# One GpSimd instruction with immediate scalars ahead of the third sequence's gathers, and two VectorE blocks exchanged in the second step

## The reference, cut to what matters

```python
emb = wte[shifted ids]                 # 16 shifts, 64 numbers each
h = tanh(emb.reshape(.., 1024) @ w1 + b1)        # 64 columns
h = h @ w2 + b2                                  # 1024 columns ("logits")
h = h + attn(layernorm(h))             # autocorrelation, top 6 lags, softmax, shifted sums
h = h + layernorm(h) @ W.T + bias + low-rank update (16 experts of rank 16)
```

## Time and profile before

| | us |
|---|---|
| median of 3 runs | 404.94 |
| these three runs | 403.80, 404.94, 409.43 |
| the profiled execution, its own time | 404.97 |
| its span, first to last instruction | 403.1 |
| PE busy in the span | 382.9 (95%) |
| DVE busy | 276.5 (69%) |
| ACT busy | 246.3 (61%) |
| POOL busy | 214.2 (53%) |

### The profile page before, as it was taken

The page is one execution under the profiler, slowest core; times in us unless marked ns, Lnnn a source line. Parts: engine busy times, 40 slices in busy tenths (PEclk is TensorE's granted clock), DMA queues, the critical chain, the costliest instruction groups (busy, mean ns, idle before and its releaser), DMA issues.

```text
span 403.1 us, 6527 instructions
## 1 busy us (share of the span) xinstructions
PE 382.9 (95%) x1908; PEld 278.7 (69%) x1908; DVE 276.5 (69%) x602; ACT 246.3 (61%) x362; POOL 214.2 (53%) x283
## 2 busy tenths in 40 slices
PE   2999699999999999999999999999999999999992
PEld 1554377777777777777777777777777777777661
DVE  2745438686777778686858677777858686866751
ACT  2524267676766675776667676667677666764641
POOL 6774626657374737466574737473856654412200
PEclk9999879999999999999999999999999999999998
DMA  8783005455565555555545556554565554555575
GB/s 212 238 329 118 5 17 210 161 228 179 215 227 212 196 179 213 201 211 199 230 143 228 202 218 224 195 208 163 213 217 213 182 229 149 212 204 208 211 312 213
DMA packets 27684, 79.86 MB, mean 198 GB/s; under 512 B 6186, under 2 KB 7482, under 8 KB 27668
## 3 DMA queue, kind: packets, MB, share of 16 engines
q1 hardware_dynamic: 22960, 75.18, 48.4%
q0 software_dynamic: 4096, 4.20, 4.8%
q10 hardware_dynamic: 612, 0.27, 0.4%
HBM read 12.40 MB, written 67.12 MB: 197 GB/s over the span
## 4 chain that ended last, share of the span: by engine, by line
PE 85%; POOL 5%; issue 3%; DMA 2%; DVE 2%; ACT 0%; DVEq 0%; POOLq 0%
PE o_ps L1092 46%; PE conv_ps L1183 14%; PE o_ps L1118 7%; PE conv_ps L1189 7%; POOL gathered L403 4%; PE sum_ps L1157 2%; PE sum_ps L1131 2%; PE et_ps L1137 2%; PE mix_ps L1169 2%; PE sum_ps L1169 2%; PE et_ps L1147 2%; DMA gathered<-in_wte,idx_now 1%; DMA ids_sb<-in_ids 1%; DVE obuf L711 1%; PE conv_ps L1077 0%
## 5 line engine op out<-in xcount | busy, mean ns | idle before, releaser
L403 POOL DMA_INDIRECT gathered<-in_wte,idx_now x128 | 127.4, 996 | 44.2 <-issue 34.4
L511 ACT ACTIVATE obuf<-o_ps,mean_sb,a_sb 128x512 f32<-128x512 f32 x128 | 99.7, 779 | 74.8 <-PE o_ps L1118 46.5
L711 DVE TENSOR_SCALAR obuf<-o_ps,a_sb,mean_sb 128x512 f32<-128x512 f32 x128 | 102.4, 809 | 57.6 <-PE o_ps L1092 33.1
L1092 PE MATMUL o_ps<-w_hi,u_hi 128*128 128x512 f32 x256 | 110.2, 430 | 0.0
L1092 PE MATMUL o_ps<-w_lo,u_hi 128*128 128x512 f32 x256 | 101.2, 395 | 0.0
L1092 PE MATMUL o_ps<-w_hi,u_lo 128*128 128x512 f32 x256 | 101.2, 395 | 0.0
L1183 PE MATMUL conv_ps<-et_hl,shift_hi 128*128 128x512 f32 x256 | 67.0, 405 | 0.0
L1092 PEld LDWEIGHTS o_ps<-w_hi,u_hi 128*128 128x128 f32 x256 | 48.1, 188 | 21.2 <-issue 12.3
L1183 PEld LDWEIGHTS conv_ps<-et_hl,shift_hi 128*128 128x128 f32 x256 | 49.2, 193 | 12.8 <-issue 1.1
L431 POOL TENSOR_SCALAR var_eps<-var 128x8 f32<-128x8 f32 x16 | 3.1, 196 | 100.8 <-DVE var L840 93.4
L1092 PEld LDWEIGHTS o_ps<-w_lo,u_hi 128*128 128x128 f32 x256 | 48.1, 188 | 11.5
(11 more groups left out here) (132 smaller groups left out, 444.0 us busy)
## 6 DMA issues: line engine op xcount, KB each, us to landing
out<-obuf SPq DMA_DIRECT2D x63, 1024.0 KB, 4.0
h_all<-in_wT SPq DMA_DIRECT2D x4, 1024.0 KB, 6.5
gathered<-in_wte,idx_now POOLq DMA_INDIRECT x128
aT_sb<-in_aT SPq DMA_DIRECT2D x1, 1024.0 KB, 10.5
bfT_sb<-in_bfT SPq DMA_DIRECT2D x1, 1024.0 KB
obuf<-in_w SPq DMA_DIRECT2D x2, 256.0 KB
lagged<-xbar_twice SPq DMA_DIRECT2D x1, 512.0 KB
out<-obuf SPq DMA_DIRECT2D x1, 512.0 KB, 4.2
```

What stands on the lines that cost most here:

```text
L403: pool.indirect_dma_start(gathered[p][:, i, :], None, wte, bass.IndirectOffsetOnAxis(ap=idx_now[p][:, i:i + 1].bitcast(U32), axis=0),).the ...
L511: nc.scalar.activation(obuf[:, q, i % 2, 0:512], o_ps[:, 2 * (i % 2), :], ACT.Identity, bias=mean_sb[pc][:, i:i + 1], scale=a_sb[pc][:, i: ...
L711: nc.vector.tensor_scalar(obuf[:, q, i % 2, 512:L], o_ps[:, 2 * (i % 2) + 1, :], a_sb[pc][:, i:i + 1], mean_sb[pc][:, i:i + 1], ALU.mult, ...
L1092: last = mm(o_ps[:, 2 * (i % 2) + n, :], lhsT, rhs[:, 512 * n:512 * (n + 1)], start=(i % 2 == 0 and f == 0), stop=(i % 2 == 1 and f == len ...
```

## The change

It has four edits.

1. `minus_half` is set to 0.0 instead of -0.5, and at the start of POOL's step 1 a `tensor_scalar` makes it `0 * 1.0 - 0.5`. It stands behind the second sequence's eight gathers and ahead of the third's index copy and gathers.
2. A semaphore `half_set` orders the memset, that instruction and the first power (L433) of step 1.
3. The third sequence's gathers are split like all later ones: three ahead of the scalars, five behind the copy of `h`.
4. DVE in step 1 does `scale_h` ahead of `g_lo_halves`.

```diff
-            pool.memset(minus_half[:, :], -0.5)
+            pool.memset(minus_half[:, :], 0.0).then_inc(half_set, 1)
...
+                if in_step(1, g, u):
+                    pool.wait_ge(half_set, 1)
+                    pool.tensor_scalar(minus_half[:, :], minus_half[:, :], 1.0, -0.5, ALU.mult, ALU.add).then_inc(half_set, 1)
                 if more:
 
                     gather(a + 1, 1 - u, a)
-                    for i in range(NT if in_step(1, g, u) else 3):
+                    for i in range(3):
                         gather_rows(1 - u, i)
...
+                    if in_step(1, g, u):
+                        pool.wait_ge(half_set, 2)
                     pool.tensor_tensor(inv_std[:, :], var_eps[:, :], minus_half[:, :], ALU.pow).then_inc(scal_step, 1)
...
-                if more and not in_step(1, g, u):
+                if more:
                     for i in range(3, NT):
                         gather_rows(1 - u, i)
...
                 if in_step(1, g, u):
+                    scale_h()
                     g_lo_halves()
-                    scale_h()
```

More of the change, by code:

```diff
@@ L208, in tower_kernel @@
         zeros_set = sem("zeros_set")
+        half_set = sem("half_set")
         pads_hi = sem("pads_hi")
```

## The result

The changed kernel takes 400.39 us (median of 10 runs, 399.81 to 402.55); the kernel before, in 10 runs beside it, 403.62 us (402.29 to 409.43). The ratio is 0.9923, 95% interval [0.9899, 0.9948]: 0.8% faster, and within 2%. Forecast were 400.5 us, from 399.3 to 404.8, with 0.97 for within 2%.

What follows compares the result with a forecast made beforehand. The prediction took PE, busy 95%, to be bounded in step 1 by a 3.7 us wait for `beta` times `h`, late through POOL's stall. Gains of 4.9 less 0.4 gave 4.5 us: 404.97 to 400.5 us, range 399.3 to 404.8.

Steps and rivals of the forecast that it cites:

- stall ends: POOL, step 1: moved behind the second sequence's last gather at 25.48, the stall of 7.46 us would end at 32.94.
- PE waits for it: PE, ahead of `conv_half(1)` in step 1: a 1.0 us wait for `add_shifts(0)` replaces the 3.7 us one, at full clock.
- L1124 waits for `extra`: PE, step 2, `four_rank_terms(0)`: it comes at 52.0 and waits until 52.7 for `extra`; 0.3 to 0.4 us lost.
- gain in the profiled execution: Whole kernel: 4.9 us gained by the end of `conv_half(1)`, less 0.4 for the rows of `extra`, gives 4.5 us.
- The first rival: POOL, step 1: the load is tied to something else and stays ahead of L431; `beta` still at 42.0, 400.5 us; chance 6%.
- the load: POOL, step 1: the stall of about 7.4 us, paid once ahead of the first instruction with immediate scalars.
- The third: POOL: the load waits for issued gathers to land at 30.41, then takes 6.2 us; gain 0.4, 404.6 us; chance 10%.
- The fourth: DVE, step 1: with a late `beta` the exchange delays `add_shifts(0)`; 2.3 us lost, 407.3 us; chance 7%.
- The fifth: PE's 1.0 us pause, or fuller queues beside the rows of `extra`, cost as much as 1.6 us; 402 us; chance 7%.
- The slack of 0.7 us for `beta`: DVE, step 1: with `beta` at 42.0 the exchange costs nothing as long as `beta` comes before 42.7.
- The second rival: POOL: transfers beside the load slow it by 1 to 3 us; 402 us; chance 25%.
- if it takes the same 7.46: POOL, step 1: assumes the load takes 7.46 us in its new place too, from 25.48 to 32.94.

Runs made afterwards that it cites:

- e1: Kernel before with only the third sequence's gathers split, three ahead of the scalars and five behind: median 404.23 us, ratio 1.0016.
- e6: Changed kernel with the early `tensor_scalar` replaced by a `tensor_tensor` without numbers, `minus_half` set to -0.5 at once: 403.16 us, one execution.
- e2: Kernel before with only `scale_h` put ahead of `g_lo_halves` in step 1: 406.47 us, ratio 1.0066.
- c1: Changed kernel measured again without any edit: 400.81 us, ratio 0.9928 to the kernel before.
- e10_before_busy: Kernel before with fifteen extra matmuls that nobody reads in PE's pause of step 1: 403.07 us, ratio 0.9989.
- e9_split_busy: Kernel before with the gathers split, plus eight extra matmuls that nobody reads in PE's pause of step 1: 402.01 us, ratio 0.9949.
- e4_one_ahead: Changed kernel with one of the third sequence's gathers ahead of the scalars in step 1 instead of three: 401.03 us, ratio 0.9928 to before.
- e8_rows_first: Changed kernel with one gather ahead, `G`'s bias row done first and `add_shifts(0)` ahead of the 64 rows' low half: 400.37 us, ratio 0.9919 to before.
- e3_no_exchange: Changed kernel with `g_lo_halves` again ahead of `scale_h` in step 1: 402.73 us, ratio 0.9978 to before.
- e11_act_first: Changed kernel with ACT's two copies of the transposed w2 ahead of the first tanh: 401.23 us, ratio 0.9920 to before.
- e12_all: Changed kernel with `G`'s bias row first, two gathers ahead of the scalars and ACT's copies ahead of the tanh: 399.37 us, ratio 0.9902 to before.
- e5_early_only: Changed kernel with the split undone, all eight gathers of the third sequence ahead of the scalars: 408.99 us, ratio 1.0128 to before.

## Why the prediction was right

Its steps against the trace after:

| step | forecast | measured |
|---|---|---|
| stall ends | 32.94 | 32.70 |
| scalars start | 37.1 | 37.30 |
| `beta` ready | 42.0 | 42.53 |
| `scale_h` ends | 43.7 | 44.21 |
| `add_shifts(0)` ends | 47.6 | 47.42 |
| PE waits for it | 1.0 | 1.82 |
| `conv_half(1)` ends | 50.65 | 50.52 |
| L1124 waits for `extra` | 0.7 | 0.55 |
| L1163 of step 2 | 53.3 | 53.10 |
| gain in the profiled execution | 4.5 | 4.70 |

The reading of the earlier trace rows, a cost paid once and moved together with five gathers, held, and so did the change of what is late next. The first rival (the load stays at L431) was wrong as to the changed kernel, and right in its arithmetic: e1 shows that without the early instruction L431 starts at 36.60. It was also right that something else than immediate scalars calls for the load (e6); that made no difference, as the early instruction is arithmetic too. The third (the load waits for landed gathers and then takes 6.2 us) fell: it would have ended at 36.6, and in the changed kernel the gather queue moved nothing from 28.7 us on, 4.0 us ahead of the stall's end. The fourth was priced well, 2.7 us against 2.3 (e2), and didn't come about, since `beta` came 3.4 us ahead of the point where it decides. The fifth fell too: the clock stayed, at 1.00 in the profile and at a mean of 0.993 to 0.997 in all sixteen executions of the changed kernel.

The prediction says that edits 1 and 3 do the same work twice, and by the traces it is right: `beta` is no earlier with the early instruction than without (42.53 against 41.89 in e1). Which of the two the time needs isn't shown, since edits 3 and 4 without the early instruction weren't run.

Four terms were mis-sized, and they offset each other.

- The slack of 0.7 us for `beta` was gone. Two of the three gathers behind the load took 1.19 and 1.17 us instead of 0.95, and the first scalar 0.49 instead of 0.19; `beta` came 0.5 us late. And the start-up of this execution was quicker: G was ready at 42.00 instead of 42.76. ACT's high half was done sooner, POOL's scalars were not, and PE waited 1.82 instead of 1.0.
- That quicker start-up is no part of the change, but is in the 4.70. From G ready to the end of the span it is 403.08 - 42.76 = 360.32 before and 398.38 - 42.00 = 356.38 after, so 3.94 us of the gain lie behind that point, under the forecast 4.5. In c1 the same sum is 398.77 - 43.32 = 355.45, so 4.87: one pair of profiles doesn't settle the size.
- I took 404.97, the profiled execution, for the typical one, since it agreed with the median of three. The median of ten runs is 403.62. The gain in the medians is 3.2 us (and 3.0 for c1_changed), not 4.5. The forecast of 400.5 met 400.39 by luck, because the base was 1.3 us too high and the gain 1.3 us too large.
- Why both were off, the granted clocks tell. The prediction takes the 1.6 us that `conv_half(1)` lost at half clock as lost in every execution. The 54 executions of the kernel before that ran beside the experiments fall into three groups: a mean clock of 0.987, as in the profile (10 of them, median 405.3 us), 0.989 to 0.992 (36, median 403.7), and 0.994 or 0.995 (8, median 402.6). So the profile had caught the group that loses most.

The prediction also took 2% for about what a measurement can tell; the interval of the changed kernel reaches 0.25% to either side.

The second rival, the load slowed by transfers beside it, had a chance of 25%, and is true in part. The stall in the profiles, by where it began, with the time from SP's issue of the copies into `lagged` (L337 or L338) to the stall's end:

| kernel | begins | stall | end behind SP's issue |
|---|---|---|---|
| before | 35.65 | 7.46 | 13.69 |
| e2_exchange_only | 35.27 | 7.22 | 12.47 |
| e10_before_busy | 35.07 | 7.16 | 12.90 |
| e9_split_busy | 29.34 | 7.73 | 6.96 |
| e1_split_only | 29.02 | 7.58 | 6.36 |
| e4_one_ahead | 25.65 | 8.45 | 3.31 |
| e8_rows_first | 25.50 | 7.12 | 3.20 |
| e3_no_exchange | 25.18 | 7.61 | 3.29 |
| changed | 25.12 | 7.58 | 3.36 |
| e11_act_first | 25.12 | 8.73 | 3.66 |
| e12_all | 24.78 | 8.41 | 3.32 |
| e6_early_tt | 24.69 | 8.83 | 2.95 |
| c1_changed | 23.94 | 8.69 | 3.37 |
| e5_early_only | 23.41 | 9.09 | 3.05 |

Behind 35 us, where hardly any transfers run, it took 7.2 to 7.5 us; near 25 us, beside the weights, 7.1 to 9.1, so up to 1.9 us more. The last column says when. SP issues those copies once its stores of `xbar`, queued behind the weights, have landed. In the changed kernel the rate of all DMA engines falls to zero at about 28.7 us, and the issue follows:

```profile
29.34 0.83 SPq L338 DMA_DIRECT2D lagged<-xbar_twice  x2
```

The nine stalls that began by 25.7 us differ by 2.0 us in length, but all ended 2.9 to 3.7 us behind that issue. (The last packets of the gather queue fit less closely: they lie 3.5 to 4.8 us ahead of the end.) So it looks as if the last 3 us or so of the load come only when the weights are through; a load that is called for more than about 4 us ahead of that point ends no sooner, it only takes longer. No run moved the weights, so this is a reading of fourteen profiles and not shown by an experiment. It also says what was lucky in the forecast's "if it takes the same 7.46": in the execution that I compared with, SP's issue came only 4.2 us behind the stall's start. The Trainium skill (GPSIMD Engine Reference, Instruction dispatch) gives about 6 us for the load of fresh code: all profiles here show more, and the measured numbers hold. The rule of the Trainium skill that a DMA engine takes turns between queues (DMA: Bandwidth & Descriptors, Queues, rings and completion order) would explain the stretch; the load's own packets are in no trace, so that it is this stays argued.

## What to carry to other kernels

A stall that an engine pays once, ahead of its first instruction of a kind, helps nobody by being moved alone: with eight gathers still between it and the consumer, the early load left `beta` where it was (e5), and with five of them moved `beta` came 5.5 to 6.2 us earlier, whether the load was called for early (changed) or not (e1). An earlier operand then pays only if the next engine uses it: the exchange on DVE cost 2.7 us with a late `beta` and was worth about 2 with an early one. When a wait is removed from a kernel ordered by hand, look for the next one on the same engine and in the queue that feeds it; three of the four follow-ups here gained, by median, under a third of their estimates, one because the gathers pushed back came too late in turn. And judge by repeats: two kernels whose profiled execution was 3 us and 4 us faster than the profiled one of before were, by median, no faster and 1.2 us faster. Before a profile serves as the base, compare its mean granted clock with that of the repeats: here the base was of the group with the lowest clock, into which 10 of 54 executions fall, and e1's profile was one of 2 in 10 with the highest.

## What the runs showed of the hardware that was not expected

- The stall of 7 to 9 us stands ahead of POOL's first `tensor_tensor` as well as its first `tensor_scalar` (e6), and not ahead of memsets, copies and indirect gathers. I had taken the immediate scalars for the cause. A second pair of `MODIFY_POOL_CONFIG`, ahead of the `partition_all_reduce` near the end, is followed by such a stall too: 375.42 to 382.57 us in the profile of before.
- Filling a pause of PE with work that nobody reads made a kernel 2.2 us faster (404.23 to 402.01 us, intervals apart). Pauses of 3.66 us (before), 2.6 (e2) and 2.5 (e5) were followed by a granted clock of 0.50 in the profiles, pauses of 1.8 (changed) and 2.1 us (e1, e3) were not; the mean clocks of e1's repeats suggest that such a pause goes either way.
- The load beside the weights' transfers took up to 1.9 us longer than in quiet, and in all nine profiles in which it began by 25.7 us it ended 2.9 to 3.7 us behind SP's issue of the copies into `lagged`.
- DVE's product of `beta` and `h` in step 1 (L813 in the kernel before) took 1.07 or 1.08 us in the six profiles in which POOL's copy of `h` ran beside it, and 0.69 or 0.70 in the eight in which it didn't.
- The start-up scatters by more than the edits weigh: ACT's first tanh, which waits for the small transfer into `b_col`, began at 8.13 us in the profile of before and at 11.27 in that of e6, and G was ready between 42.0 and 45.9 us. That is why marks behind it were compared.
